# A windowed-attention block on one core: q/k/v convolution one step further ahead of its scores, the projection behind the transposes of the probabilities, and the negated mean on VectorE

## The reference, cut to what matters

```python
xw = windows of 16 x 16 of x                     # 64 windows an image
q, k, v = (shuffle_invert(conv3(xw, w, b), 2) for (w, b) in qkv)   # 3x3 convolutions, then 64 tokens x 128 features
q, k, v = (ln(t, g, b) for t in (q, k, v))       # layer norm over the 128 features of a token
attn = softmax(einsum('bhqd,bhkd->bhqk', q * SCALE, k) + bias)     # 8 heads, 64 x 64 scores
out = einsum('bhqk,bhkd->bhqd', attn, v)
out = out @ proj_w.T + proj_b
xr = windows back to the image of (xw + pixel_shuffle(out, 2))
y = xr + conv3(gelu(conv3(xr, c1w, c1b)), c2w, c2b)
```

## Time and profile before

| | |
|---|---|
| median of three runs | 831.84 us (830.34 to 832.01) |
| the profiled execution's own time | 833.53 us |
| its span, first to last instruction | 831.7 us |
| TensorE busy | 749.4 us, 90% of the span |
| VectorE busy | 659.3 us, 79% |
| ScalarE busy | 603.8 us, 73% |
| GpSimd busy | 491.9 us, 59% |
| TensorE's granted clock, mean | 0.995 of full speed |

### The profile page before, as it was taken

The page is one execution under the profiler, slowest core; times in us unless marked ns, Lnnn a source line. Parts: engine busy times, 40 slices in busy tenths (PEclk is TensorE's granted clock), DMA queues, the critical chain, the costliest instruction groups (busy, mean ns, idle before and its releaser), DMA issues.

```text
span 831.7 us, 18390 instructions
## 1 busy us (share of the span) xinstructions
PE 749.4 (90%) x5704; PEld 536.1 (64%) x5704; DVE 659.3 (79%) x2141; ACT 603.8 (73%) x1287; POOL 491.9 (59%) x1041
## 2 busy tenths in 40 slices
PE   0479999989899999999899999998989999999988
PEld 0257777767456677766656677776645677776753
DVE  5548888987868888888867888898776888887575
ACT  1388888877567888886737888877747788887840
POOL 5356776763346777765436776775335677776410
PEclk9999999999999999999999999999999999999999
DMA  7111160100112132100111216100011213000002
GB/s 256 58 30 30 31 230 5 53 2 1 58 64 90 36 120 111 58 1 1 59 39 52 71 30 230 58 2 1 7 52 65 96 30 130 0 1 1 2 1 101
DMA packets 17643, 47.00 MB, mean 57 GB/s; under 512 B 2080, under 2 KB 2720, under 8 KB 17568
## 3 DMA queue, kind: packets, MB, share of 16 engines
q1 hardware_dynamic: 17568, 46.09, 16.2%
HBM read 37.69 MB, written 8.39 MB: 55 GB/s over the span
## 4 chain that ended last, share of the span: by engine, by line
PE 46%; DVE 23%; issue 11%; POOL 10%; ACT 9%; DMA 1%; DVEq 0%; SPq 0%; ACTq 0%; POOLq 0%
PE y_ps L1011 11%; PE o_bank L1090 6%; PE s_ps L1065 4%; PE pt_ps L1078 4%; POOL ln_rs L724 4%; DVE h_lo L506 3%; DVE ln_st L542 3%; PE ox_ps L1034 3%; DVE h_hi L503 3%; PE s_ps L1124 3%; ACT qk_n L856 3%; PE ox_ps L1124 3%; PE o_bank L1124 3%; PE pt_ps L1124 3%; PE t_ps L1045 2%
## 5 line engine op out<-in xcount | busy, mean ns | idle before, releaser
L856 ACT ACTIVATE qk_n<-y_ps,ln_nr,ln_rs 128x128 f32<-128x128 f32 x256 | 103.7, 459 | 94.7 <-POOL ln_nr L727 94.0
L737 POOL TENSOR_TENSOR sc<-sc,mx 128x512 f32<-128x512 f32 x128 | 133.7, 1045 | 39.2 <-DVE mx L577 39.2
L1011 PE MATMUL y_ps<-w_hi,x_hi 128*128 128x192 f16 (+1 forms) x512 | 148.4, 290 | 0.0
L1011 PE MATMUL y_ps<-w_hi,x_lo 128*128 128x192 f16 (+1 forms) x512 | 148.1, 289 | 0.0
L1011 PE MATMUL y_ps<-w_lo,x_hi 128*128 128x192 f16 (+1 forms) x512 | 148.0, 289 | 0.0
L562 DVE TENSOR_TENSOR sc<-s_ps,biasS 128x512 f32<-128x512 f32 x128 | 86.8, 678 | 54.9 <-PE s_ps L1065 53.7
L1090 PE MATMUL o_bank<-v_bd,pt 128*128 128x66 f32 x1024 | 129.3, 269 | 0.0
L1090 PEld LDWEIGHTS o_bank<-v_bd,pt 128*128 128x128 f32 x1024 | 125.2, 193 | 0.2
L542 DVE BATCH_NORM_STATS2 ln_st<-y_ps 128x6 f32<-128x128 f32 x384 | 88.9, 287 | 42.9 <-PE y_ps L1011 41.1
L720 POOL TENSOR_TENSOR ln_ve<-ln_mv,eps_y 128x3 f32<-128x3 f32 x128 | 33.8, 264 | 148.2 <-DVE ln_mv L547 148.0
L724 POOL TENSOR_TENSOR ln_rs<-ln_ve,neg_half 128x3 f32<-128x3 f32 x128 | 113.3, 885 | 10.7
(11 more groups left out here) (181 smaller groups left out, 1612.4 us busy)
## 6 DMA issues: line engine op xcount, KB each, us to landing
xs<-in_x_sh_dram SPq DMA_DIRECT2D x32, 576.0 KB, 4.2
xst<-in_x_al_dram SPq DMA_DIRECT2D x16, 512.0 KB, 8.0
xf<-in_x_al_dram SPq DMA_DIRECT2D x32, 256.0 KB, 5.3
out_dram<-xf SPq DMA_DIRECT2D x32, 256.0 KB, 2.0
wst<-in_wqkv_dram SPq DMA_DIRECT2D x1, 768.0 KB, 4.2
w1s<-in_w_dram SPq DMA_DIRECT2D x1, 256.0 KB, 8.8
w2s<-in_w_dram SPq DMA_DIRECT2D x1, 256.0 KB, 8.8
biasS<-in_bias_t_dram SPq DMA_DIRECT2D x1, 256.0 KB, 9.7
```

The lines of the kernel that those rows point to most:

```text
L737: pool.tensor_tensor(sc[i % 4][:, :, :, :], sc[i % 4][:, :, :, :], mx[i % 2][:, :, :].unsqueeze(2).to_broadcast([P, HP, TOK, 2]), ALU.subt ...
L856: ins = act.activation(qk_n[j][:, t, :].rearrange("p (h y x) -> p h y x", h=HEADS, y=2), by_head(y_ps[j][:, E * t:E * (t + 1)]), ACT.Identity,
L1011: ins = pe.matmul(y.rearrange("p (t e) -> p t e", t=3)[:, :, cols], xx[r % 2][:, s, a % 2, 2 * TS * (a // 2):2 * TS * (a // 2 + TS)], ww[: ...
```

## The change

The convolution of a pair, its statistics, scales and normalisation come one step earlier on all engines: a step i now does them for pair i + 5, and the head begins at step -5. The first two tiles of c2 and their results are spread over one step more. TensorE's projection comes behind the transposes of the probabilities of its step (step 35 apart), and VectorE's addition of it to xr comes behind the copy of the transposed probabilities. VectorE computes the negated mean, behind the moments, and tells GpSimd by a semaphore. The handling of a new row of x comes two steps earlier (scaling, borders), the high halves one step and the low halves one step earlier.

```diff
-        HEAD = range(-4, 4)
+        HEAD = range(-5, 4)
...
-        c2_in = {-4: (0, 1), -3: (2,), -2: (3,), -1: (4,), 0: (5,), 1: (6,), 2: (7,)}
-        result_in = {-3: (0, 1), -2: (2,), -1: (3,), 0: (4,), 1: (5,), 2: (6,), 3: (7,)}
+        c2_in = {-5: (0,), -4: (1,), -3: (2,), -2: (3,), -1: (4,), 0: (5,), 1: (6,), 2: (7,)}
+        result_in = {-4: (0,), -3: (1,), -2: (2,), -1: (3,), 0: (4,), 1: (5,), 2: (6,), 3: (7,)}
...
@@ VectorE, step @@
-                if has(i + 4):
-                    m = i + 4
+                if has(i + 5):
+                    m = i + 5
...
                     ins.then_inc(ln_moments, 1)
+                    v.wait_ge(ln_moments, p0 + (m + 1))
+                    v.tensor_scalar(ln_nm[m % 2][:, :], ln_mv[m % 2][:, :, 0], -1.0, None, ALU.mult).then_inc(
+                        ln_negated, 1)
...
-                if i % 4 == 3 and i >= 7:
-                    r = (i - 7) // 4
-                    v.wait_ge(proj_done, r0 + (r + 1))
...
                     v.tensor_copy(pt[m % 2][:, :, :], pt_ps[:, :, :]).then_inc(pt_copied, 1)
+                if i % 4 == 3 and i >= 7:
+                    r = (i - 7) // 4
+                    v.wait_ge(proj_done, r0 + (r + 1))
...
-                if i % 4 == 3 and 2 <= (i + 9) // 4 < NROW:
-                    row((i + 9) // 4, r0)
+                if i % 4 == 1 and 2 <= (i + 11) // 4 < NROW:
+                    row((i + 11) // 4, r0)
...
@@ GpSimd, step @@
-                    pool.tensor_tensor(ln_ve[j][:, :], ln_mv[j][:, :, 1], eps_y[:, :], ALU.add)
-                    pool.tensor_scalar(ln_nm[j][:, :], ln_mv[j][:, :, 0], -1.0, None, ALU.mult).then_inc(
+                    pool.tensor_tensor(ln_ve[j][:, :], ln_mv[j][:, :, 1], eps_y[:, :], ALU.add).then_inc(
                         ln_var_eps, 1)
...
                     pool.wait_ge(ln_pow, p0 + (m + 1))
+                    pool.wait_ge(ln_negated, p0 + (m + 1))
...
-                    for z in ((), (0,), (1,), ())[i % 4]:
+                    for z in ((0,), (1,), (), ())[i % 4]:
                         low((i + 8) // 4, z, p0, r0)
...
@@ ScalarE, step @@
-                if i % 4 == 3 and 2 <= (i + 9) // 4 < NROW:
-                    row((i + 9) // 4, r0, rr0)
-                if 2 <= (i + 8) // 4 < NROW and i % 4 < 2:
-                    high((i + 8) // 4, i % 4, p0, r0)
+                if i % 4 == 1 and 2 <= (i + 11) // 4 < NROW:
+                    row((i + 11) // 4, r0, rr0)
+                if 2 <= (i + 9) // 4 < NROW and (i + 1) % 4 < 2:
+                    high((i + 9) // 4, (i + 1) % 4, p0, r0)
...
-                if has(i + 4):
-                    m = i + 4
+                if has(i + 5):
+                    m = i + 5
...
@@ TensorE, step @@
-                if has(i + 4):
-                    m = i + 4
+                if has(i + 5):
+                    m = i + 5
...
-                if i % 4 == 3 and i >= 7:
-                    r = (i - 7) // 4
-                    pe.wait_ge(ot_copied, r0 + (r + 1))
-                    pe.matmul(ox_ps[:, :], projg[:, :], ot[r % 2][:, :], start=True, stop=True).then_inc(
-                        proj_done, 1)
+                if i == PAIRS + 3:
+                    project(i, r0)
...
                     ins.then_inc(ptr_done, 1)
+
+                if i % 4 == 3 and 7 <= i < PAIRS:
+                    project(i, r0)
```

More of the change, by code:

```diff
@@ L203, in conv_attention @@
         ln_scales = sem("ln_scales")
+        ln_negated = sem("ln_negated")
         ln_v_scales = sem("ln_v_scales")
@@ L548, in step @@
                     ins.then_inc(ln_moments, 1)
-                if last is not None and i == -4:
+                    v.wait_ge(ln_moments, p0 + (m + 1))
+                    v.tensor_scalar(ln_nm[m % 2][:, :], ln_mv[m % 2][:, :, 0], -1.0, None, ALU.mult).then_inc(
+                        ln_negated, 1)
+                if last is not None and i == HEAD.start:
                     for t in range(BORDER1, T1N):
@@ L584, in step @@
                     v.tensor_copy(pt[m % 2][:, :, :], pt_ps[:, :, :]).then_inc(pt_copied, 1)
-                if i % 4 == 3 and 2 <= (i + 9) // 4 < NROW:
-                    row((i + 9) // 4, r0)
+                if i % 4 == 3 and i >= 7:
+                    r = (i - 7) // 4
+                    v.wait_ge(proj_done, r0 + (r + 1))
+                    if i == 7:
+                        v.wait_ge(xr_begun, b * 4 + 5)
+                    rows = xr[:, bass.ds((row0 + r) * TS, TS), :].rearrange("p i (w j) -> p w i j", w=NWIN)
+                    v.tensor_tensor(rows, rows, ox_ps[:, :].rearrange("p (w i j) -> p w i j", w=NWIN, i=TS),
+                                    ALU.add).then_inc(xr_added, 1)
+                if i % 4 == 1 and 2 <= (i + 11) // 4 < NROW:
+                    row((i + 11) // 4, r0)
                 if has(i - 2):
@@ L983, in c1, with project @@
                 ins.then_inc(c1_done, 1)
+            def project(i, r0):
+                r = (i - 7) // 4
+                pe.wait_ge(ot_copied, r0 + (r + 1))
+                pe.matmul(ox_ps[:, :], projg[:, :], ot[r % 2][:, :], start=True, stop=True).then_inc(proj_done, 1)
             def by_feature(m, p0, r0, last=None):
@@ L1017, in step @@
                 if last is not None:
-                    if i == -4:
+                    if i == HEAD.start:
                         c1(last, 11)
```

## The result

The changed kernel takes 851.88 us (median of 4 runs, 850.97 to 853.24) against 831.4 us for the kernel before (830.34 to 832.01): a ratio of 1.0249 [1.0228, 1.027]. It is slower by 20.5 us. The profiled execution took 852.79 us, and its span grew from 831.7 to 850.9 us: 19.2 us to be accounted for.

The account below looks back on a forecast made before the run. TensorE was taken to set the pace. Four images x (2.19 - 0.5) = 6.76, three heads x 1.63 = 4.89 and the first head's 1.2 gave +12.9 us: 845 us, range 831 to 858.

Parts of the forecast that it names:

- The projection behind the transposes: Steps with a projection: transposes still wait for ScalarE's exponential, then the projection runs uncovered; +0.96 a group, +4.80 an image.
- step 3: Score step with i modulo 4 = 3, holding the projection; forecast to go from 5.19 to 6.15 us.
- step 2: Score step with i modulo 4 = 2, first of a group of four; 4.04 us without a gap.
- Five steps ahead: Steady part: TensorE's wait for normalised q and k in step 1 goes; -2.61 us an image.
- step 1: Score step with i modulo 4 = 1; forecast to lose a wait of 0.61 to 0.78 us and take 4.04.
- One more convolution in the head: Heads: one convolution more, with TensorE never free; +1.63 us in each of three, +1.2 in the first.
- The tail: Step 27, without its convolution, and what follows: -0.5 us an image, bounds 0 and -1.63.
- The negation: Negated mean on VectorE: 0.15 to 0.23 us a step, covered by waits; nothing in the sum.
- 855: Rival: convolution waits for v's normalisation in its PSUM bank, so step 1's wait only moves; 855 us, chance 0.05.
- 856: Rival: VectorE and GpSimd become the chain, the negation's 0.19 lying on three steps a group; 856 us, chance 0.11.
- The faster rival: Rival: the transposes of step 3 don't wait, and it takes 4.88 us; 819 us, chance 0.15.

Follow-up runs that it names:

- e5: Changed kernel with ScalarE's exponential ahead of q, k and v normalised in steps with i modulo 4 = 2: 821.69 us, 0.989.
- e1: Changed kernel with the projection and VectorE's addition of it back in their old places: 834.42 us, 1.0035.
- e2: Kernel before, still four steps ahead, with only the projection behind the probabilities' transposes and its addition behind the copy of pt: 843.77 us, 1.0156.
- e12: Changed kernel with early exponential, c1's first tile in step 27, and pair 1's convolution ahead of c2's first tile: 815.32 us, 0.9815.
- e13: Changed kernel with dead work added in step 27, the last pair's convolution done once more: 847.66 us, 1.0197.
- e4: Changed kernel with the negated mean back on GpSimd: 853.97 us, 1.0278.
- e9: Kernel before, four steps ahead, projection in its old place, with the exponential first in steps with i modulo 4 = 2: 854.35 us, 1.0279.
- e14: Kernel before with only the first tile of c1 in step 27 instead of 28: 841.79 us, 1.0118.
- e6: Changed kernel with the first tile of c1 in step 27 instead of 28: 840.22 us, 1.0115.

## Why the prediction was right, and where it was off

- **The projection behind the transposes** (+0.96 a group) was right in mechanism and nearly in size: step 3 was to be 6.15 us and is 6.04, with the transposes 7.89 us after step 2 began where 7.90 was forecast. e5 shows the cause: moving the exponential, and nothing of TensorE, moves the transposes. e1 gives its price in the whole kernel, 17.5 us; four images of 4.80 are 19.2.
- **Five steps ahead** (-2.61 an image): step 1 is 4.04 us as forecast, and the steady part is right, but not because of the lead alone. e2 shows that the projection's move would have taken that wait as well. The two edits' gains do not add; the prediction's sum, which counted the wait once, does not depend on whose it was.
- **One more convolution in the head** (+1.63): the third image's head, from its first convolution to that of step 4, went from 47.68 to 49.67 us, +1.99. TensorE was not without a free moment there, as the working had it from 20 us of the head: c2's first tile waits 1.50 us in the kernel before and 1.51 in the changed one, and in e12, where the convolution fills that wait, the head is 1.31 us shorter. With the steady part's 4.01 - 1.99 = 2.02 for the 2.19 forecast, the two errors partly cancel. The first image's +2.70 stands for 3.39, within what that stretch varies.
- **The tail** (-0.5 an image, bounds 0 and -1.63) is the term that failed: +0.83 to +1.35. The working had step 27's wait right: the transposes come 582.54 - 573.11 = 9.43 us after step 26 began, in the forecast's own way. It did not ask what TensorE's clock does where the missing convolution leaves a wait in front of L1052 and another in front of L1085. The third image's +1.35 less the 1.92 us of the slow stretch is -0.57; for the four, 4.49 - 7.06 = -2.57, -0.64 an image. Apart from the clock the term was near, and e13's first tail shows that share by itself. The term is 6.5 us of the 7 that the forecast of 845 lies short, so that the forecast was right in the range but had nothing in it for the clock.
- **The negation** entered at nothing, and e4 found nothing in the time (in the trace, -0.14 us a group and +0.4 a head). The overlap lost, 0.15 to 0.23 us a step in the working, shows: the scores' addition (L566) starts 101.19 - 101.07 = 0.12 us behind the moments' end, where it started 0.08 ahead of it, 0.20 together, and it is covered. VectorE's busy time rose from 34.51 to 36.24 of 40 us.
- **The rivals.** The time lies close to those of two rivals, 855 and 856, but neither is what happened. Steps 0, 1 and 2 are 4.16, 4.04 and 4.04 us, so VectorE and GpSimd are not the chain; and no convolution of the steady part waits, so the lead is there. The faster rival needed transposes 6.63 us after step 2's start. In the changed kernel they start at 7.89 to 8.38 in every step 3. In e5, with the early exponential, they come at 6.63 in one step 3 of each image, the first (i = 7), and at 6.90 to 7.13 in the other four.

## What to carry to other kernels

Work that stands in front of a wait covers it: before moving it behind, find what ends the wait on the other engine and whether that can be made earlier; here the same move cost 18.5 us with the exponential last in ScalarE's list and won 5 with it first. A longer lead need not pay by the wait it removes (here another edit removed the same wait); it pays by the orders and early buffers that it makes possible, which e9 and e14 show failing without it. Where a pipeline runs out of work, look at the granted clock of that stretch, and put the next stage's work there.

## What was not expected of the hardware

**The clock at the end of the windows.** TensorE's granted clock fell towards the 1.2 GHz level behind waits of 1.43 and 1.92 us in the changed kernel, and stayed at the upper level through a wait of 1.93 in e6. The same wait had both outcomes in one execution: e14 has 2.75 us in each of its four images, and the clock stayed behind the third (busy 2.25 of 5 us) and fell behind the others (0.66 to 0.72 in a slice of 5 us); e13 kept it behind one image of four. It can fall in the steady part as well: in e6 step 23 of the first image takes 8.20 us, with 0.78 in a slice, and 6.54 in the other images. What decides it stays open; what it costs is in the rows, 1.39 to 2.03 us for each tail of the changed kernel.

**A tiny instruction held up for 0.8 us.** VectorE of the changed kernel in a step of the second image's head:

```profile
255.91 0.80 DVE L551 TENSOR_SCALAR ln_nm<-ln_mv 128x3 f32<-128x3 f32 x1
```

GpSimd at that time:

```profile
255.54 1.16 POOL L706 TENSOR_TENSOR x_lo<-xnf,x_hi 128x512 f16<-128x512 f32 x1
```

The negation takes 0.17 us as a rule, and 0.80 to 0.84 in 4 of its 128 places, where it runs beside GpSimd's L706 and ends 255.91 + 0.80 = 256.71, as L706 does (256.70). (In three more places it starts 0.08 us before L706 ends and takes its 0.17.) The Trainium skill, SBUF — State Buffer, "SBUF: two separate sides", has an exclusive lock for whoever starts first between a GpSimd instruction and a VectorE instruction that runs in a two-port mode or reads two SBUF tensors. The trace agrees as far as it goes: here it is VectorE that waits to the end, where in the earlier trace rows GpSimd did. That the negation, with one input, runs in a two-port mode is not shown by any run here. Beside ln_ve, the case that the prediction asked about, there is no loss: ln_ve (L724) takes 0.192 us in the mean over its 128 places, and 0.204 at most.
